# Attention kernel on one NeuronCore: the output product as three products of high and low parts, and the transposes of q and k at other places of a pair

## What is computed

```python
q, k, v = split(x @ w_qkv)                # 256 -> 3 * 1024
q, k = l2norm(q) * q_scale, l2norm(k) * k_scale
# windows of 128 queries; keys and values of the window before, its own and the next; rotary on q and k
attn = softmax(where(window_mask, NEG, q @ k.T))
out = (attn @ v) @ w_out                  # 1024 -> 256
x = layernorm(x + out)
```

## Time and profile before

| | |
|---|---|
| median of 3 runs | 3116.45 us (3114.57 to 3116.84) |
| profiled execution | 3117.74 us, of which the profile's span 3115.9 us |
| attention, to its last store | 1940 us of the span |
| busy over the span | PE 95%, DVE 76%, ACT 69%, POOL 53% |
| granted TensorE clock, mean | 0.988 of full speed |

### The profile page before, as it was taken

One profiled execution on the slowest core, in us unless ns is written; L12 is line 12 of the kernel. 1 busy time (PEld: TensorE's weight loads), 2 busy tenths in 40 slices (PEclk: granted clock), 3 DMA queues, 4 the chain that ended last, 5 costly groups with the idle time before them and its releaser, 6 DMA issues. The chain is left out here.

```text
span 3115.9 us, 56168 instructions
## 1 busy us (share of the span) xinstructions
PE 2972.7 (95%) x18095; PEld 2381.2 (76%) x18095; DVE 2360.4 (76%) x6841; ACT 2164.3 (69%) x5670; POOL 1658.1 (53%) x2226
## 2 busy tenths in 40 slices
PE   7999999999999999999999997699999999999996
PEld 6777777777777777777777775478888888888885
DVE  6877877877877877877877875787777777777775
ACT  5666766766766766765766764477888888888884
POOL 5655655655655654654655654334555555555555
PEclk9999999999999999999999999799999999999998
DMA  2000000000000000000000001200000000000000
GB/s 83 8 15 21 8 15 21 8 15 15 15 15 15 15 15 15 15 15 15 15 15 15 8 21 36 74 14 8 14 15 14 15 21 21 14 15 15 8 15 21
DMA packets 51202, 57.23 MB, mean 18 GB/s; under 512 B 3008, under 2 KB 48592, under 8 KB 50912
## 3 DMA queue, kind: packets, MB, share of 16 engines
q1 hardware_dynamic: 47904, 50.67, 5.0%
q10 hardware_dynamic: 3008, 2.98, 0.3%
HBM read 36.86 MB, written 16.78 MB: 17 GB/s over the span
## 5 line engine op out<-in xcount | busy, mean ns | idle before, releaser
L614 POOL TENSOR_SCALAR a_ex<-a_ex,a_rc 128x384 f32<-128x384 f32 (+1 forms) x1024 | 531.4, 532 | 713.8 <-DVE a_rc L525 713.7
L420 ACT ACTIVATE a_ex<-a_sm,a_nm 128x384 f32<-128x384 f32 (+1 forms) x1024 | 572.2, 560 | 67.3 <-DVE a_nm L518 55.1
L518 DVE CUSTOM_DVE_ANT_0 a_sm<-sc,a_mask,a_rn 128x384 f32<-128x384 f32 (+1 forms) x1024 | 530.4, 544 | 9.3 <-PE sc L292 9.3
L426 ACT ACTIVATE a_pt<-tp 128x256 f32<-128x256 f32 (+1 forms) x512 | 220.0, 430 | 306.4 <-PE tp L309 306.2
L261 PE MATMUL pj<-a_whi,a_xhi 128*128 128x384 f32 x1024 | 391.6, 382 | 7.2 <-DVE a_wlo L187 4.2
L1681 POOL TENSOR_TENSOR b_alo<-b_ring,b_ahi 128x512 fp32r<-128x512 f32 x128 | 169.4, 1323 | 412.0 <-DVE b_ring L1510 373.4
L598 POOL TENSOR_TENSOR a_qr<-a_ra,a_rb 128x256 f32<-128x256 f32 x512 | 369.3, 735 | 12.2 <-DVE a_rb L498 9.0
L261 PE MATMUL pj<-a_whi,a_xlo 128*128 128x384 f32 x1024 | 348.0, 340 | 0.0
L261 PE MATMUL pj<-a_wlo,a_xhi 128*128 128x384 f32 x1024 | 347.2, 339 | 0.0
L292 PE MATMUL sc<-a_kT,a_qT 64*128 64x384 f32 (+1 forms) x2048 | 345.2, 455 | 1.4 <-DVE a_pt L530 0.7
L318 PE MATMUL qk<-a_pt,a_v 128*64 128x384 f32 (+1 forms) x2048 | 303.9, 437 | 26.1 <-DVE a_pt L530 23.9
(11 more groups left out here) (233 smaller groups left out, 8046.3 us busy)
## 6 DMA issues: line engine op xcount, KB each, us to landing
a_xres<-x SPq DMA_DIRECT2D x16, 512.0 KB, 3.9
y<-a_res SPq DMA_DIRECT2D x16, 512.0 KB, 2.9
b_y<-y SPq DMA_DIRECT2D x16, 512.0 KB, 3.8
a_xin<-x SPq DMA_DIRECT2D x15, 512.0 KB, 4.0
out<-b_y SPq DMA_DIRECT2D x15, 512.0 KB, 2.9
a_xin<-wqkv SPq DMA_DIRECT2D x8, 256.0 KB, 2.8
a_stage<-wqkv SPq DMA_DIRECT2D x3, 384.0 KB, 10.0
a_ot<-wqkv ACTq DMA_DIRECT2D x3, 384.0 KB, 12.5
```

Source lines behind the costliest of these rows:

```text
L420: e.activation(ex[h][w][:, 0:width], sm[h][w % 2][:, 0:width], ACT.Exp, bias=nm[:, w, h:h + 1], scale=-1.0, accum_out=rs[:, w, h:h + 1]).t ...
L426: e.activation(pt_window(0, w), blocks(TP, w), ACT.Copy).then_inc(g['pt_act'], 1)
L518: e.tensor_tensor_reduce(out=sm[h][w % 2][:, 0:width], in0=SC[w % 2][h][:, 0:width], in1=mem['mask'][:, off:off + width], scale=rn[:, par, ...
L614: e.tensor_scalar(row, row, 0.0, rc[:, w, h:h + 1], ALU.add, ALU.mult).then_inc(g['exn_pool'], 1)
```

## The change

1. **Output product.** `ot` (fp32) becomes `ohi` and `olo` (fp32r), `wo` becomes `wo_hi` and `wo_lo`. ScalarE's evacuation of the values now writes `ohi`. A new VectorE instruction for each pair, `dve_o_low`, subtracts it from the bank `qk` and gives `olo`. The product is three fp32r matmuls where it was one of fp32. Whoever waited for ScalarE's `ot_act` to reuse `qk` waits for `ol_dve`.
2. **Order in the half u = 0.** On TensorE the transposes of q move behind the weights' transpose of window `i`, head 0, and half a projection; those of k move behind the transpose of window `i + 1`, head 0. On ScalarE the copy of k moves behind the copy of the weights of window `i + 1`.
3. **Buffers.** Masked scores are written straight into `ex` and the exponential runs in place; `sm` and its wait go. x for the residual is loaded into `res` itself, after the maxima and the store of the sequence before; `xres` goes.
4. **Weights.** `wo` is loaded in two pieces by way of `res`, and split in the first body: two ScalarE copies at the ends of (3,1) and (5,1), four GpSimd subtractions in pairs 4 and 6. The raw qkv weights get a buffer of their own name that `ohi` and `olo` lie over. In the last body one store and one load of SyncE's queue move behind two loads of weights.

```diff
     def pe_q_transpose(e, n, m, par):
         e.wait_ge(g['rot_pool'], TT * m + TT)
         if due(n):
-            e.wait_ge(g['ot_act'], n)
+            e.wait_ge(g['ol_dve'], n)
...
         for t in range(2):
+            tokens = slice((2 * k + t) * P, (2 * k + t + 1) * P)
             for c in range(HC):
-                last = e.matmul(QK[:, t * DIM:(t + 1) * DIM], ot[:, c, (2 * k + t) * P:(2 * k + t + 1) * P],
-                    wo[:, c, :], start=c == 0, stop=c == HC - 1)
+                for j, (rows_t, weight) in enumerate(((ohi, wo_hi), (olo, wo_hi), (ohi, wo_lo))):
+                    last = e.matmul(QK[:, t * DIM:(t + 1) * DIM], rows_t[:, c, tokens], weight[:, c, :],
+                        start=c == 0 and j == 0, stop=c == HC - 1 and j == 2)
...
         if u == 0:
-            if at.has_pair(1):
-                pe_q_transpose(e, n, n + 1, (p + 1) % 2)
             pe_transpose_weights(e, i, w, 0, at.has_next())
             if at.has_pair(2):
                 pe_project(e, seq, n + 2, pair, w, 0)
+            if at.has_pair(1):
+                pe_q_transpose(e, n, n + 1, (p + 1) % 2)
+            if at.has_pair(2):
                 pe_project(e, seq, n + 2, pair, w, 1)
             pe_transpose_weights(e, i, w, 1, at.has_next())
+            pe_transpose_weights(e, i + 1, w + 1, 0, at.has_next())
             if at.has_pair(1):
                 pe_k_transpose(e, n + 1, (p + 1) % 2)
-            pe_transpose_weights(e, i + 1, w + 1, 0, at.has_next())
...
-        e.activation(ot[:, p, :], QK[:, :], ACT.Copy).then_inc(g['ot_act'], 1)
+        e.activation(ohi[:, p, :], QK[:, :], ACT.Copy).then_inc(g['ot_act'], 1)
...
+            act_evacuate_weights(e, i + 1, w + 1)
             if at.has_pair(1):
                 act_k_evacuate(e, n + 1, (p + 1) % 2)
-            act_evacuate_weights(e, i + 1, w + 1)
...
+    def dve_o_low(e, n, p):
+        e.wait_ge(g['ot_act'], n + 1)
+        e.tensor_tensor(olo[:, p, :], QK[:, :], ohi[:, p, :].bitcast(F32), ALU.subtract).then_inc(g['ol_dve'], 1)
...
-        if due(2 * i + h - 3):
-            e.wait_ge(g['e_act'], 2 * i + h - 3)
-        e.tensor_tensor_reduce(out=sm[h][w % 2][:, 0:width], in0=SC[w % 2][h][:, 0:width],
+        e.tensor_tensor_reduce(out=ex[h][w][:, 0:width], in0=SC[w % 2][h][:, 0:width],
...
         if ahead:
             dve_mask_max(e, next_i, par, next_w, 0)
+        if u == 0 and at.has_pair(-1):
+            dve_o_low(e, n - 1, (p - 1) % PAIRS)
+        if ahead:
             dve_mask_max(e, next_i, par, next_w, 1)
```

More of the change, by code:

```diff
@@ L429, in act_o_evacuate @@
         e.wait_ge(g['pv_pe'], n + 1)
-        if n in RAW_UNDER:
-            e.wait_ge(g['wl_dve'], RAW_UNDER[n])
-        e.activation(ot[:, p, :], QK[:, :], ACT.Copy).then_inc(g['ot_act'], 1)
+        if n == 0:
+            e.wait_ge(g['wl_dve'], 3)
+        if n in (0, 3):
+            e.wait_ge(g['wl_pool'], 5 if n else 3)
+        e.activation(ohi[:, p, :], QK[:, :], ACT.Copy).then_inc(g['ot_act'], 1)
     def act_next_weights(e, k):
@@ L482, in act_half @@
             act_weights_high(e, 3 + p // 2)
+        if at.first and (at.at(3, 1) or at.at(5, 1)):
+            act_out_weights(e, p // 4)
         if w1_piece(at) is not None:
@@ L535, in dve_residual @@
             e.wait_ge(g['x_keep'], 16 * (seq + 1))
-            if due(seq):
-                e.wait_ge(g['y_out'], 16 * seq)
-        e.tensor_tensor(halves(mem['res'], k), QK[:, :], halves(mem['xres'], k), ALU.add).then_inc(g['op_dve'], 1)
+        e.tensor_tensor(halves(mem['res'], k), QK[:, :], halves(mem['res'], k), ALU.add).then_inc(g['op_dve'], 1)
     def dve_stats(e, seq, k):
@@ L547, in dve_amax @@
         col = TT * seq + t
-        e.tensor_reduce(mem['amax'][:, col:col + 1], mem['res'][:, t, :], AX.X, ALU.max, apply_absolute_value=True)
+        last = e.tensor_reduce(mem['amax'][:, col:col + 1], mem['res'][:, t, :], AX.X, ALU.max,
+            apply_absolute_value=True)
+        if t == TT - 1:
+            last.then_inc(g['am_dve'], 1)
     def dve_half(e, at):
@@ L636, in pool_half @@
             pool_weights_low(e, 3 + p // 2)
+        if at.first and p in (4, 6):
+            pool_out_weights(e, p // 6, u)
         if w1_piece(at) is not None:
@@ L651, in keep @@
             def keep(seq):
-                e.wait_ge(g['op_dve'], 2 * seq)
-                e.dma_start(mem['xres'][:, :, :], x_tiles[seq]).then_inc(g['x_keep'], 16)
+                if seq:
+                    e.wait_ge(g['am_dve'], seq)
+                    e.wait_ge(g['y_out'], 16 * seq)
+                else:
+                    e.wait_ge(g['wo_pool'], 4)
+                e.dma_start(mem['res'][:, :, :], x_tiles[seq]).then_inc(g['x_keep'], 16)
             def store(seq):
@@ L679, in _ @@
             for k in range(W1_COUNT):
+                if k == 2:
+                    store(B - 2)
+                    keep(B - 1)
                 if k >= 2:
@@ L786, in sb @@
         return stack.enter_context(nc.sbuf_tensor('a_' + name, shape, dt))
-    mem = {k: sb(k, v) for k, v in dict(scales=[P, 2, DH], rot=[P, TT, 4, DH], stage=[P, 3 * HD], wo=[P, HC, DIM],
-        ot=[P, PAIRS, S], mask=[P, 3 * WS], half=[P, TT * 4], xin=[P, TT, DIM], xres=[P, TT, DIM], res=[P, TT,
+    mem = {k: sb(k, v) for k, v in dict(scales=[P, 2, DH], rot=[P, TT, 4, DH], mask=[P, 3 * WS], half=[P, TT * 4],
+        xin=[P, TT, DIM], res=[P, TT,
             DIM], ra=[P, 2, 2 * PW], rb=[P, 2, 2 * PW],
@@ L791, in attention_memory @@
         rc=[P, NW, 2], **Norm.buffers('ln1')).items()}
+    with ExitStack() as first:
+        mem['raw'] = first.enter_context(nc.sbuf_tensor('a_raw', [P, DC, 3 * HD], F32))
+    mem['ohi'], mem['olo'] = (sb(k, [P, PAIRS, S], F32R) for k in ('ohi', 'olo'))
+    mem['wo_hi'], mem['wo_lo'] = (sb(k, [P, HC, DIM], F32R) for k in ('wo_hi', 'wo_lo'))
     mem['whi'], mem['wlo'] = (sb(k, [P, DC, 3 * HD], F32R) for k in ('whi', 'wlo'))
@@ L800, in attention_memory @@
     mem['pt'] = [pt[:, h, :, :] for h in range(2)]
-    for k, n in dict(sm=2, ex=4).items():
+    for k, n in dict(ex=4).items():
         mem[k] = [[sb(f'{k}{h}{i}', [P, 3 * WS]) for i in range(n)] for h in range(2)]
```

43 lines of the change are left out of this document (29 added, 14 removed).

## The result

The changed kernel takes **3172.26 us** (median of 5 runs, 3168.44 to 3173.69), the kernel before 3116.3 us (5 runs, 3112.09 to 3116.84). The ratio is 1.0182, with a 95% interval from 1.0168 to 1.0196: **slower by 1.8%**, some 56 us, inside the predicted range and 4 us from the predicted 3176.

What follows compares the result with a forecast made beforehand. Two nearly level loops bound it: TensorE's (12.7 us) and VectorE with ScalarE (12.37). Fourteen bodies +51.5, first +4.5, last +5.4, tail -1.9 give +59.5 us: 3176 as a median, range 3125 to 3200 (8 in 10).

Steps and rivals of the forecast that it cites:

- The output product: Output blocks on TensorE: 48 fp32r matmuls, 5.72 us a block for 7.01 and 6.91, saving 2.48 us a body.
- The loop: VectorE, TensorE and ScalarE in u = 0: subtraction delays copy of q by 0.91 us, second window's exponential by 0.92.
- The turns: Windows of the eight pairs in a body, from +1.06 us in pair 1 to -1.90 in pair 0, together +3.68.
- Pair 5: Turn with x on both engines: no slack, so 13.22 to 14.14 us, +0.92.
- Pair 6: Turn where TensorE ends last: +0.5 us, as the scores of u = 1 are late by 0.58.
- The 0.14 us: Plain turn, u = 1: transposes that VectorE's fourth instruction waits for come 0.14 us after VectorE is ready.
- First body: No maxima or statistics, so +2.8 us; two ScalarE copies of 128x1024 between squares and VectorE, +1.7.
- Last body: Seven pairs of the last body, before its tail: +5.4 us.
- The end: Tail of the last body: two blocks give back 2.6 us, last subtraction and its signal take 0.74; -1.9.
- TensorE alone: Rival: VectorE and ScalarE absorb the subtraction, so the product's gain counts in full, 39 us, to 3077; chance 0.12.
- Only the 0.61 counts: Rival: subtraction costs only its 0.61 us on VectorE, the wait is covered; some +16 us, 3132; chance 0.17.
- More than I count: Rival: waits shift TensorE's work in u = 1, 0.15 to 0.3 us more a turn; 3195 to 3214; chance 0.15.

Runs made afterwards that it cites:

- the product alone: Changed kernel without the subtraction (second product takes the high part again, same 48 matmuls a block) and with the old order in u = 0: 3079.83 us.
- high copy and subtraction in the second half: Changed kernel, old order, subtraction on GpSimd; ScalarE's fp32 copy stays in u = 0, rounding copy and subtraction mostly move to u = 1: 3094.93 us.
- pair 0's subtraction in the idle time: Kernel with late GpSimd subtraction, with pair 0's moved from half (1,1) to (2,0), behind the rotation of q: 3095.56 us.

## Why the prediction was right, and where it was not

**The output product.** Predicted 2.48 us a body, and the kernel with the product alone is 118.53 − 116.05 = 2.48 shorter. That the two agree to the last digit is luck. The blocks themselves were a little dearer than the 5.72 of the sum: 398.43 to 404.28 = 5.85, and 405.92 to 411.75 = 5.83, as the first product of a block takes 0.20 to 0.22 us to the next and the rest 0.12. Two blocks save 2.24 of 13.92 us. Pair 0 as a whole gains 2.35 (26.50 to 24.15), and the other 0.1 us, 13.03 to 12.98 in pairs 3 and 4, are the masks' buffers and not the product.

**The loop.** This was the step on which the size of the loss hung, and every link of it is in the rows: the copy of q comes 0.96 us late (0.91 predicted), the exponential 0.97 (0.92), the scores of u = 1 0.64 (0.58). The idle times that were named stand there too, 0.28 on VectorE (126 such waits) and 0.15 on TensorE in pair 0 (88 waits, up to 1.6 us). TensorE's wait is not the 0.3 us in nearly all pairs that was named, but anything from none to 1.33, by the pair. The sum allowed about 0.06 us from the subtraction's end to the start of the transposes; it measures 0.14, and that is the 0.05 by which the copy is later than predicted. TensorE's busy share of attention was put at 93%; it went from 96.3% (1868.4 of 1940 us) to 93.8% (1870.6 of 1995). The kernel with the subtraction one place ahead shows that the place makes the larger part of the price.

**The turns.** Pair 1 +0.96 (predicted +1.06), pair 2 +0.55 (+0.66), pairs 3 and 4 +0.92 and +0.91 (+0.92), pair 7 +0.54 (+0.60), pair 0 −1.73 (−1.90). Two terms were off by more. **Pair 5** was put at +0.92 and measures +0.67: VectorE used to wait 0.17 us there for ScalarE's high part of x, and no longer does, as it comes late itself. The prediction took that pair to have no slack, and none of its rows shows that pair's waits. **Pair 6** was put at +0.5 and measures +0.67. The 0.14 us that the sum adds to a turn without maxima has no row behind it, and pairs 1, 2 and 7 came out 0.06 to 0.11 lower. In pair 0, +0.51 is left beside the blocks' −2.24. The errors cancel in part: the body has +3.49 for a predicted +3.68, and 14 of them +49.3 us for +51.5 (1659.08 to 1708.42 us, values to values).

**First body.** Predicted +4.5, measured −0.4; here the term was wrong, and for a reason that I had not looked for. In the kernel before, pairs 1 and 3 of the first body ran with a lower granted clock:

```profile
44.95:61.20 16.25, 14.21 (x84) 11.15 (x85) 12.40 (x36) 9.60 (x33) 10.34 (x15) 0.89 0.00 1
74.74:91.05 16.31, 14.19 (x85) 11.20 (x85) 12.38 (x36) 9.85 (x33) 10.43 (x15) 0.90 0.01 2
```

```profile
50.45 0.75 PE L272 MATMUL qk<-s_ident,a_qr 128*128 128x128 f32 x3 [1.86 <-POOL a_qr L598]
```

TensorE waits 1.86 us for GpSimd's rotated q (the second fence, from its timeline), and then works at half speed for about 4 us: the granted clock is 0.50 from 52 to 53 us, and its projection products start 0.32 us apart and not 0.17 to 0.18, as they do from 55.3 us on. In the changed kernel the same pairs are at full clock:

```profile
44.13:58.85 14.72, 12.88 (x84) 9.52 (x85) 12.75 (x37) 9.50 (x33) 10.37 (x15) 1.00 0.00 0
73.32:88.13 14.81, 12.89 (x84) 9.52 (x85) 12.76 (x37) 9.58 (x33) 10.44 (x15) 1.00 0.01 2
```

The new order seems to do this: with it alone the pair takes 14.17 us at 1.00 and TensorE waits 0.97 us in one piece, since it has other transposes and half a projection to do first. In the old order with the product alone it is 16.22 at 0.89. Of the profiled executions, all five in the new order have a short pair 1 in the first body (14.17 to 14.72 us), and six of the eight in the old order a long one (16.22 to 16.79). The two others, with high copy and subtraction in the second half and with pair 0's subtraction in the idle time, had the same wait of 1.86 us, kept their clock and took 14.65 and 14.66. So the order is not the whole reason, and the clock is worth 1.6 us a pair here, 3.2 us in all. Another 0.8 us of the miss lie ahead of the first values (44.95 and 44.13 us); the rest wasn't followed.

**Last body.** Predicted +5.4, measured +7.44. Here the clock goes the other way:

```profile
1948.05:1963.30 15.25, 11.94 (x61) 7.12 (x61) 11.01 (x32) 9.16 (x31) 9.18 (x15) 0.78 0.16 48
```

```profile
1953.69 0.63 PE L289 MATMUL qk<-s_ident,a_qr 128*128 128x128 f32 x4 [1.62 <-DVE a_olo L538]
1955.10 1.02 PE L296 MATMUL qk<-s_ident,a_qr 128*128 128x128 f32 x4 [0.24 <-DVE a_qT L534]
```

Pair 6 of the last body has fewer projections, TensorE idles longer, and the pair takes 15.25 us at clock 0.78 (12.43 at 1.00 before). The prediction gave it the turn of any other body. The kernel with the extra VectorE instruction and the fp32 product has the same two waits there (1.61 and 0.24 us) and keeps its clock:

```profile
1986.68:2000.07 13.39, 9.33 (x61) 5.63 (x61) 10.92 (x32) 9.17 (x31) 9.34 (x15) 1.00 0.15 41
```

So 1.86 us of the 2.0 that the term missed are the clock's.

**The end** was put at −1.9 and came out at −1.8. The whole profiled difference is −0.4 + 49.3 + 7.4 − 1.8 = 54.5 of 54.6 us. The first body missed by −4.9, the fourteen by −2.2, the last by +2.0: that the median came within 4 us of the middle is in part luck, and the clock has its share in it on both sides.

**The rivals.** TensorE alone (3077) is what the product alone gives, 3079.8: the condition was that no engine waits, and they do. "Only the 0.61 counts" (3132) is what the kernel with the subtraction one place ahead took, 3133.3: there its condition nearly holds, as TensorE waits for the subtraction 19 times in place of 88, and pair 3 takes 13.58. In the changed kernel the pair of 13.95 us rules it out. "More than I count" did not come: only pairs 6 and 0 took more than the sum gave them, 0.17 us each. And where the texts of the experiments erred, it was mostly on one term: the order alone, 29.5 and not 54 us, because pair 1 hides it whole and pairs 3 and 4 in part. In the prediction this term was never priced alone, only the loop's whole delay, and so the error didn't reach the sum.

## What to carry to other kernels

Before you add an instruction to an engine with 20% of idle time, write down the circle in which it stands: who waits for it, and which instruction of its own engine waits for that one. What it costs is the delay of the last link (0.96 us here for 0.61 of work), and the same instruction one place further ahead can cost far less (25 us here and not 64), and on an engine outside the circle nothing in the steady state. When a long matmul becomes cheaper by more parts, price the making of the parts at the place where they are made, 128 times, not the product alone.
